# Values of five quads in seven products of 256 columns, in one rhythm with the key products

## The reference

```python
x = _rmsnorm(hidden_states, ln_weight)          # of the normalised x
h_q = (x @ w_q.T).reshape(b, lq, H, DH)
h_k = (key_value_states @ w_k.T).reshape(b, lk, H, DH)
h_v = (key_value_states @ w_v.T).reshape(b, lk, H, DH)
score = softmax(einsum('bqhd,bkhd->bhqk', h_q, h_k) + position_bias, masked)
attn = jnp.einsum('bhqk,bkhd->bqhd', score, h_v)
return hidden_states + attn @ w_out.T
```

## Time and profile before

| | us |
|---|---|
| median of 3 runs | 1605.64 (1605.09 to 1606.79) |
| profiled execution | 1605.11 |
| its span, first to last instruction | 1603.3 |
| PE busy | 1595.0 |
| PEld busy | 1364.4 |
| DVE / POOL / ACT busy | 995.6 / 878.4 / 748.2 |

### The profile page before, as it was taken

The page is one execution under the profiler, slowest core; times in us unless marked ns, Lnnn a source line. Parts: engine busy times, 40 slices in busy tenths (PEclk is TensorE's granted clock), DMA queues, the critical chain, the costliest instruction groups (busy, mean ns, idle before and its releaser), DMA issues.

```text
span 1603.3 us, 25022 instructions
## 1 busy us (share of the span) xinstructions
PE 1595.0 (99%) x8512; PEld 1364.4 (85%) x8512; DVE 995.6 (62%) x1528; ACT 748.2 (47%) x1922; POOL 878.4 (55%) x688
## 2 busy tenths in 40 slices
PE   9999999999999999999999999999999999999999
PEld 7888888888888888888888887888898898889887
DVE  7533233736676666666779667767656656665675
ACT  5522221335554544545544334656555556564553
POOL 6444444446665664664669775554536435443435
DMA  9544444422332333333231111111110111010011
GB/s 348 175 159 151 150 150 154 157 85 93 113 121 96 123 115 104 120 108 108 99 141 49 57 41 51 60 34 46 40 34 27 47 40 33 28 47 27 15 53 53
DMA packets 52111, 146.44 MB, mean 91 GB/s; under 512 B 7264, under 2 KB 12000, under 8 KB 51520
## 3 DMA queue, kind: packets, MB, share of 16 engines
q1 hardware_dynamic: 52032, 145.41, 26.0%
HBM read 107.64 MB, written 37.75 MB: 91 GB/s over the span
## 4 chain that ended last, share of the span: by engine, by line
PE 96%; DVE 2%; POOL 1%; ACT 1%; DMA 0%; issue 0%; SPq 0%; DVEq 0%
PE banks L55 27%; PE banks L57 27%; PE banks L56 27%; PE banks L788 4%; PE banks L808 4%; PE banks L2299 4%; PE banks L797 2%; PE banks L2306 2%; PE banks L224 1%; DVE resid L1949 0%; DMA rawA<-in_x_wK 0%; PE banks L733 0%; DMA g_swapped<-in_l_b 0%; DVE g_q L2599 0%; POOL g_swapped L2763 0%
## 5 line engine op out<-in xcount | busy, mean ns | idle before, releaser
L2763 POOL TENSOR_TENSOR g_swapped<-g_swapped,rawB 128x512 f32<-128x512 f32 x80 | 103.1, 1291 | 171.2 <-ACT g_swapped L2445 171.2
L1542 POOL TENSOR_TENSOR x_probs<-x_probs,x_inv 128x512 f32<-128x512 f32 x64 | 66.6, 1040 | 170.3 <-DVE x_inv L1328 167.6
L1065 ACT ACTIVATE x_probs<-x_probs,x_top 128x128 f32<-128x128 f32 x256 | 99.5, 390 | 92.2 <-DVE x_top L1319 92.2
L1444 POOL TENSOR_TENSOR wtA_lo<-rawA,wtA_hi 128x1024 fp32r<-128x1024 f32 (+1 forms) x31 | 72.0, 2324 | 97.1 <-ACT wtB_hi L970 75.9
L1204 DVE COPY c_v_kept<-banks 128x512 f32<-128x512 f32 x64 | 44.1, 690 | 107.8 <-PE banks L57 107.8
L2757 POOL TENSOR_TENSOR g_probs<-g_probs,g_inv 128x512 f32<-128x512 f32 x64 | 67.7, 1079 | 74.5 <-DVE g_inv L2584 74.4
L2593 DVE TENSOR_TENSOR g_turned_by<-banks,rawB 128x512 f32<-128x512 f32 x80 | 55.2, 690 | 85.8 <-ACT g_swapped L2445 85.8
L55 PE MATMUL banks<-wtV_hi,g_att_lo 128*128 128x512 f32 x256 | 104.3, 407 | 0.0
L55 PE MATMUL banks<-xT_hi,wtO_lo 128*128 128x512 f32 x256 | 102.9, 402 | 0.0
L2444 ACT COPY g_swapped<-banks 64x512 f32<-64x512 f32 x80 | 46.7, 583 | 120.3 <-PE banks L57 113.6
L56 PE MATMUL banks<-wtV_lo,g_att_hi 128*128 128x512 f32 x256 | 100.3, 392 | 0.0
(11 more groups left out here) (353 smaller groups left out, 5146.3 us busy)
## 6 DMA issues: line engine op xcount, KB each, us to landing
kept_k<-c_k_kept SPq DMA_DIRECT2D x16, 1024.0 KB, 4.0
x_k<-kept_k SPq DMA_DIRECT2D x32, 512.0 KB, 4.4
kept_v<-c_v_kept SPq DMA_DIRECT2D x14, 1024.0 KB, 4.9
x_v<-kept_v SPq DMA_DIRECT2D x28, 512.0 KB, 3.5
rawA<-in_x_wQ SPq DMA_DIRECT2D x16, 512.0 KB, 4.5
rawO<-in_x_wO SPq DMA_DIRECT2D x16, 512.0 KB, 3.5
rawO<-in_g_wQ SPq DMA_DIRECT2D x16, 512.0 KB, 3.5
rawV<-in_g_wO SPq DMA_DIRECT2D x16, 512.0 KB, 3.5
```

Source lines behind the costliest of these rows:

```text
L1065: e = nc.scalar.activation(probs[:, b, :], probs[:, b, :], ACT.Exp, bias=top[:, b:b + 1], accum_out=total[:, b:b + 1])
L1444: return pool.tensor_tensor(wt[into][1][:, cut], raw[kind][:, cut], f32(wt[into][0][:, cut]), ALU.subtract)
L1542: pool.tensor_tensor(probs[:, part, :], probs[:, part, :], rows, ALU.mult).then_inc(probs_ready, 1)
L2763: pool.tensor_tensor(part, part, sin[:, :].unsqueeze(1).to_broadcast([P, HB, P]), ALU.mult)\
```

## The change

Quads of rounds 1 to 5 (`FOLDED` = 5) get their values by seven products, too. In `folded_half` each half of a round makes the values of four batches from seven parts (`value_part`). A part is 2 batches x 2 chunks x 3 products = 12 matmuls, with 256 moving columns (two heads). Parts and key products stand in one rhythm: three key products, three value parts, two and two, two and two. Quad 0, quad 6 (round 6) and quad 7 keep the units of 512 columns; in round 6 three value units stand after the last key products as before.

Weights: DVE makes four combinations (`value_combine`, `value_combine_more`), ACT their high parts, and DVE the low parts of three of them (`second_third_low`, `fourth_low`); these three live in `xT`, which x leaves free until round 6; the others stand in `wtV` and `wtO` as before. The sums that Strassen's method needs are made by DVE (`value_sums`, five a half) and copies by ACT (two a half). The whole preparation of x (`turn_x`, `centre`, `scale_x`, `high`, `x_low`, `add_hidden`) moves to round 6, two transposed batches between units. POOL's `mask_of` moves to `first_pair`. POOL's `combine` and `seven_low`, ACT's `seven_weights` and the waits quoted above are not touched. Core of the diff:

```diff
+            def value_part(bank, w, x, j, adds=False):
+                for e in range(2):
+                    for k in range(2):
+                        mm = product(pe, banks[:, 4 + bank, 2 * P * e:2 * P * (e + 1)],
+                                     [t[:, k, tok(2 * j + e)] for t in x], [t[:, k, :] for t in w],
+                                     e == 0 and k == 0 and not adds, k == 1, adds or e == 1)
+                mm.then_inc(vo_made, 1)
-            def seven_keys(i, which):
+            def key_start(i, which):
                 n = key_step(i, which)
                 weights_ready("A", 2 + n + 1)
...
+            def folded_half(i, j):
+                m = key_step(i, j)
+                very_first = isinstance(i, int) and i == 1 and j == 0
+                key_start(i, j)
+                if j == 0:
+                    weights_ready("V", i + 1)
...
+                value_part(X, va11, c11, j)
+                if j == 0:
+                    pe.wait_ge(ctx_lo, CTX_PARTS + 2 * i - 1)
...
+                value_part(Y, vs2, ct2, j)
+                value_part(Z, vs1, ct1, j)
+                key_middle(i, j)
...
+                value_part(Y, vs3, ct3, j, True)
+                if j == 0:
+                    weights_ready("O", i + 1)
...
+                value_part(X, va12, c21, j, True)
+                key_end(i, j)
...
+                value_part(Y, va22, ct4, j, True)
...
+                value_part(Z, vs4, c22, j, True)
...
+            def second_third_low(i):
+                dve.wait_ge(ctx_hi, CTX_PARTS + 2 * i - 1)
+                dve.tensor_tensor(xT[1][:, 0, :], centred[:, 0:2, :].rearrange("p n d -> p (n d)"), f32(xT[0][:, 0, :]),
+                                  ALU.subtract).then_inc(ctx_lo, 1)
...
+                        if j == 0:
+                            second_third_low(i)
+                        first()
+                        if j == 0:
+                            fourth_low(i)
```

More of the change, by code:

```diff
@@ L450, in context_rounds @@
             body(1)
-            with engine.Fori(2, QUADS - 2) as i:
+            with engine.Fori(2, QUADS - 3) as i:
                 body(i)
+            body(QUADS - 3)
             body(QUADS - 2)
@@ L696, in seven_keys, with key_end @@
                 part(Y, s3, ct3, True)
[L697 to L702, removed]
+            def key_end(i, which):
+                n = key_step(i, which)
                 pe.wait_ge(q_sums, 5 * n + 2)
@@ L1029, in context_round @@
                     return
-                second = isinstance(i, int) and i == 1
+                if not isinstance(i, int) or i < QUADS - 2:
+                    for j in range(2):
+                        m = key_step(i, j)
+                        more = j == 1 and (not isinstance(i, int) or i < FOLDED)
+                        key_copy(i, j)
+                        value_copy(i, j)
+                        key_quarter(i, j)
+                        if more:
+                            folded_weights(i + 1, "V", group_made(m) + 3)
+                        if more:
+                            second_third_high(i + 1, group_made(m) + 4)
+                        value_quarter_copy(i, j)
+                        key_weights(m + 1)
+                        if more:
+                            folded_weights(i + 1, "O", group_made(m) + 6)
+                            fourth_high(group_made(m) + 7)
+                    return
@@ L1043, in context_round @@
+                high(1)
                 key_weights(key_step(i, 0) + 1)
[L1044 to L1049, removed]
-                    for b in range(4, 7):
-                        add_hidden(b)
-                    high(7)
-                    add_hidden(7)
+                scale_x(4)
+                scale_x(5)
+                high(2)
@@ L1054, in context_round @@
+                high(3)
+                scale_x(6)
+                scale_x(7)
+                for b in range(4, B):
+                    high(b)
                 key_copy(i, 1)
                 key_quarter(i, 1)
-                if isinstance(i, int) and i == QUADS - 2:
-                    last_key_weights()
-                else:
-                    key_weights(key_step(i, 1) + 1)
+                for b in range(B):
+                    add_hidden(b)
+                last_key_weights()
             def exps(n, j):
@@ L1294, in context_round @@
-                if second:
-                    dve.wait_ge(mask_in, DMA)
-                    dve.tensor_reduce(some[:, :], mask8, AX_X, ALU.max).then_inc(mask_ready, 1)
+                if not isinstance(i, int) or i < QUADS - 2:
+                    for j in range(2):
+                        more = j == 1 and (not isinstance(i, int) or i < FOLDED)
+                        first, next_two, last_two = key_sums(i, j)
+                        value_first, value_next, value_last = value_sums(i, j)
+                        if j == 0:
+                            second_third_low(i)
+                        first()
+                        if j == 0:
+                            fourth_low(i)
+                        if more:
+                            value_combine(i + 1)
+                        value_first()
+                        if more:
+                            value_combine_more(i + 1)
+                        next_two()
+                        value_next()
+                        last_two()
+                        value_last()
+                    return
@@ L1298, in query_twist @@
+                twist.summed(dve, 1, 0, 0)
+                for b in range(5, B):
+                    keep(b)
+                    if b == 5:
+                        twist.summed(dve, 3, 0, 1)
+                        twist.summed(dve, 2, 1, 1)
+                dve.wait_ge(mask_in, DMA)
+                dve.tensor_reduce(some[:, :], mask8, AX_X, ALU.max).then_inc(mask_ready, 1)
             def query_twist():
```

300 lines of the change are left out of this document (207 added, 93 removed).

## The result

| | before | after |
|---|---|---|
| median, us | 1605.37 (1604.77 to 1606.79, 4 runs) | 1639.82 (1639.05 to 1640.54, 4 runs) |
| ratio, 95% interval | | 1.0212 [1.0198, 1.0225] |
| profiled execution, us | 1605.11 | 1640.54 |
| its span; mean granted clock | 1603.3; 1.00 | 1638.7; 0.991 |

The account below looks back on a forecast made before the run. PE, busy throughout the context rounds, was taken as the bound. Columns -8.0, waits +26.6, first folded quad +0.6 and transposes -0.3 gave +18.9 us on 1605.11, 1624.0, stated as 1624.5 us for the median; range 1619 to 1632.

Parts of the forecast that it names:

- The bound, and what is paid in full: Context rounds 1 to 6: PE has no idle time to win, so every new wait is paid in full.
- Columns, -8.0: Five folded quads: 96 matmuls of 512 columns become 168 of 256 at 0.120 us, gaining 1.60 us a quad, 8.0 us.
- The cover, ten waits of 2.66, +26.6: After each folded half: key weights ready 5.32 us after the seventh product, PE arrives at 2.88; ten waits, +26.6 us.
- First folded quad, +0.6: PE waits once for wtV's low part, which POOL finishes late because of DVE's new operation, +0.6 us.
- Lock at the boundaries: POOL's wtB_lo starts 0.3 us before DVE, costing nothing; rival: the other order, 1.2 us at five places, 1630.5 us, 10%.
- Moved or hidden work at nothing: Moved x preparation, value sums, copies, stores and POOL's mask operation stay hidden behind PE and are costed at nothing.
- the bound that was kept for round 6: Moved x work in round 6 might slip by at most one value unit, 2.7 us; 3 us allowed upward.
- The waits set the clock back: Rival: the first product after each of ten waits runs at half speed, 1.36 us more each, 1638 us; 7%.
- POOL's waits for ACT wtB_hi much shorter than 9 us: Sign expected in the trace: POOL's waits for ACT's copy of wtB_hi, 9.36 us before, become much shorter.
- A folded quad: Sign expected on PE's timeline: a folded quad lasts 2 x (9.52 + 10.08 + 2.66) = 44.5 us against 40.8 before.

Follow-up runs that it names:

- experiment 7: Experiment 1 with ACT's key copy before the scalings of x and DVE's first key sum before centrings and, in the first folded quad, low parts; 1598.96 us.
- experiment 4: The changed kernel plus 18 matmuls of 256 columns, read by nobody, at the end of each folded half; 1627.29 us, ratio 1.0135.
- experiment 1: The changed kernel with PE's order altered so that four value parts instead of two follow the seventh product; 1600.58 us, ratio 0.9967.
- experiment 6: The changed kernel with separate semaphores for wtA: POOL starts wtA_lo earlier, PE's first key product waits for wtA alone, the second for wtB; 1604.84 us.
- experiment 5: The changed kernel with 5 unread matmuls of 256 columns (0.60 us) at the end of each folded half; 1637.39 us, ratio 1.0203.
- experiment 3: The kernel before, 512-column units only, with one value unit instead of three behind the seventh product in rounds 2 to 5; 1637.3 us, ratio 1.0195.
- experiment 2: The changed kernel with three value parts instead of two behind the seventh product; 1612.63 us, ratio 1.0042.

## Why the prediction was wrong

*The bound, and what is paid in full*: right. No idle time stood in the stage, and every wait showed in the time.

*Columns, -8.0*: right in kind, 0.7 us too much. The parts go at 0.120 us a matmul, as said, but the key products of 512 columns between them start 0.229 us apart on average (experiment 7) instead of 0.2267; why stays open. The gain is 7.3 us. The Trainium skill's formula (TensorE: Matmul & The Clock Gate, "Back-to-back issue gap"), which the page gives for a matmul by itself, would have made it 11.9 us for the columns, and no run came to that.

*The cover, ten waits of 2.66, +26.6*: right in its place and number, and in size to about 1 us. Ten stops in the trace, 26.6 us in all, but that is without the restarts, for which the forecast had 25.8 (10 x 2.58); between experiments 4 and 1, restarts included, it is 27.8. With one part more behind the seventh product the stops are halved, with two more gone. Four are a little shorter than 2.58 (2.50 to 2.55), six longer (2.72 to 2.79): there PE starts 0.34 us after POOL's end, where I had 0.14 from one place.

*First folded quad, +0.6*: 0.4. *Lock at the boundaries*: DVE came late, as said, and POOL kept its 1.80:

```profile
95.08 1.80 POOL L1733 TENSOR_TENSOR wtB_lo<-rawB,wtB_hi 128x768 fp32r<-128x768 f32 x1
96.84 3.35 POOL L1650 TENSOR_TENSOR wtV_lo<-rawV,wtV_hi 128x1024 fp32r<-128x1024 f32 x1
```
```profile
95.32 2.65 DVE L1395 TENSOR_TENSOR xT_lo<-s_centred,xT_hi 128x1024 fp32r<-128x1024 f32 x1
```

POOL was first by 0.24 us (0.3 forecast), and DVE's 1.2 us of work lasted 2.65. So that rival did not happen. What I did not say is the second row: the next POOL operation then seems to stand behind DVE, 3.35 us instead of 2.4. It is hidden here and costs 0.45 us a quad in experiment 6.

*Moved or hidden work at nothing*: right for the changed kernel. That held because the stops gave slack: where they are gone, experiments 1 and 6, ACT's key copy behind the scaling of x costs 1.7 us, inside the bound that was kept for round 6.

***The waits set the clock back: the step that failed.*** The sum has the clock at nothing behind all ten waits, and that is the term that was wrong: it cost 14.5 us in the trace, and 12.5 between experiment 4 and the change. It was the rival with 7%, and it is what happened. Its mechanism and price were nearly right: 10 x 1.36 = 13.6 forecast; the lower level lasts for six to eight matmuls where six were assumed, and the first stop was spared. What failed is the chance. I had a row that said nothing on stops of 2.5 us (the longest was 0.85, at clock 1.00) and let "12% of the stage idle" stand in for one. No row tied the clock to a share of idle time, and none of these runs does; experiment 5 shows stops of 2.2 and of 1.9 us in one kernel coming out differently. The row at the start was weak evidence of the lower level: the small matmuls are slower there, but the view has clock 1.00 for the first 5 us of that trace. The Trainium skill (same page, "HAM oscillation — how this bites in real kernels") tells of a kernel in which waits between bursts, of some 3 to 5 us, do this each time. The trace agrees for nine of ten stops, and these are shorter, 2.50 to 2.79 us; I had given that page's case too little. Both ends of an unknown cost must be carried into the range: with nothing to tell 0 from 13.6 us, it should have reached 1638 and somewhat beyond. The columns (0.7) and the slow start of the profiled execution (1.4) are the rest of what the forecast lacks.

*What would show it*: "POOL's waits for ACT wtB_hi much shorter than 9 us" was wrong by thought alone. They became longer, 10.76 in the row above, since POOL's work per half quad is the same and the half quad has grown. It does not bear on the time. A folded quad was given as 44.5 us; from 145.44 to 193.50 it is 48.1 us: 44.5, two slow stretches (3.2) and stops a little longer than forecast.

**Still open** is what decides whether one given stop between 2 and 2.9 us brings the clock down. Shown is: of ten such stops in the change nine did, in experiment 3 five of eight, in experiment 5 six of ten (counting those of 1.9), in experiment 2 and 4, with stops of at most 1.56 us, none. The total without any clock loss can be read from experiment 4: its profiled execution took 1627.24 us where the forecast has 1624.0 for one. Of these 3.2 us the stops and restarts make 1.5 (28.1 instead of 26.6), the columns 0.5, the wait in round 6 with its restart 0.5, and the start 0.5 (8.90 instead of 8.41); the wait in the first folded quad is 0.2 us shorter than forecast, which leaves some 0.4 us that I can't place. Open, too, is why PE starts 0.34 us behind POOL at some places and 0.10 at others.

## What to carry to other kernels

Before a step is cut into smaller ones, find the longest chain that hangs on its last instruction, and compare it with the work that then follows it, not with the period of the loop: here 5.46 us of casts and subtractions had a cover of 8.16 and got 2.88, and moving two parts behind it, with no instruction added or removed, is worth 39 us. Stops of TensorE like those of 2.1 us or more here, behind 20 of 24 of which the clock fell, should be priced with a slow restart on top (1.6 us here); where the trace has no stop of that length, both ends go into the range. And when waits go away, look again at everything that was late but hidden behind them: each removal here let the next one out, 1.7 us in round 6 and 0.45 us a quad.

## What the hardware showed that I had not expected

- The granted clock fell behind 20 stops of 2.14 to 2.93 us between stretches of some 20 us in which PE was never idle, for 6 to 14 matmuls of 512 columns, mostly seven (0.427 us each instead of 0.2267). It did not behind 28 others of the same places: ten of 1.10 to 1.56 us, ten of 0.39 to 0.70, four of 1.91 to 1.97, and four among those of 2.50 to 2.93 (one in the change, three in experiment 3).
- Filling a stop with matmuls that nobody needs made the kernel 12.5 us faster.
- Where a DVE operation with two inputs in SBUF starts while POOL works, both can pay in turn: DVE took 2.65 us instead of the 1.2 that it takes alone, beside POOL's 1.80 (POOL had begun 0.24 us earlier), and POOL's next operation then took 3.35 us instead of 2.4. In the first folded quad, where DVE began 0.57 us before POOL (52.91 and 53.48), DVE took 1.22 us and POOL 2.91.
